# A scan solved by rounded and exact iterations: two rounded and one exact iteration per block in place of two and two, with another order inside a turn

## The reference

```python
def _mlp(params, h):
    W1, b1, W2, b2 = params
    return jax.nn.silu(h @ W1 + b1) @ W2 + b2
...
def step(params, kvt):
    k_t, v_t = kvt
    g = jax.grad(loss_fn)(params, k_t, v_t)
    new_params = tuple((p - LR * gp for p, gp in zip(params, g)))
    return (new_params, None)
params, _ = jax.lax.scan(step, (W1, b1, W2, b2), (k, v))
q = x @ W_Q
return _mlp(params, q)
```

## Time and profile before

| | |
|---|---|
| median of 3 runs | 483.13 us (482.81 to 485.1) |
| the profiled execution's own time | 484.08 us |
| its span, first to last instruction | 481.9 us |
| PE busy | 430.7 us, 89% of the span |
| DVE, ACT, POOL busy | 280.8, 245.1, 243.1 us |
| granted clock of PE, mean | 0.947 of full |
| turns of the scan | from 177.48 us (parameters of turn 0) to 327.6 us |

### The profile page before, as it was taken

The page is one execution under the profiler, slowest core; times in us unless marked ns, Lnnn a source line. Parts: engine busy times, 40 slices in busy tenths (PEclk is TensorE's granted clock), DMA queues, the critical chain, the costliest instruction groups (busy, mean ns, idle before and its releaser), DMA issues.

```text
span 481.9 us, 9866 instructions
## 1 busy us (share of the span) xinstructions
PE 430.7 (89%) x2875; PEld 356.0 (74%) x2875; DVE 280.8 (58%) x1031; ACT 245.1 (51%) x617; POOL 243.1 (50%) x369
## 2 busy tenths in 40 slices
PE   7899899999908989999999999999799799999940
PEld 5444699999903679899999989974644499999930
DVE  4945455555528646677777777754965245555514
ACT  3594355555410445556556565544696145555520
POOL 4367777545500344555555546552247777554530
PEclk9799999999957999999999999999989999999985
DMA  8981334100075200000000000000001417110028
GB/s 231 260 278 56 113 104 151 37 26 25 18 186 175 41 1 0 3 2 2 1 2 1 1 2 2 3 0 1 2 23 56 112 50 205 35 34 28 20 63 216
DMA packets 34513, 30.89 MB, mean 64 GB/s; under 512 B 3838, under 2 KB 30085, under 8 KB 34464
## 3 DMA queue, kind: packets, MB, share of 16 engines
q1 hardware_dynamic: 24608, 19.17, 14.7%
q0 software_dynamic: 4544, 8.47, 5.4%
q10 hardware_dynamic: 5312, 2.62, 2.1%
HBM read 15.55 MB, written 15.61 MB: 65 GB/s over the span
## 4 chain that ended last, share of the span: by engine, by line
PE 73%; DVE 8%; DMA 6%; POOL 4%; issue 4%; ACT 4%; ACTq 0%; SPq 0%; DVEq 0%; POOLq 0%
PE bank L1308 18%; PE bank L741 15%; PE bank L728 14%; POOL slots_dram L1435 3%; PE bank L599 3%; DMA stage<-y_dram 3%; PE bank L1101 2%; PE bank L689 2%; PE bank L716 2%; PE bank L1178 2%; DMA stage<-slots_dram 2%; PE bank L1139 1%; DVE stats L419 1%; PE bank L699 1%; PE bank L1162 1%
## 5 line engine op out<-in xcount | busy, mean ns | idle before, releaser
L1692 DVE TENSOR_TENSOR sq<-bank,relu 128x512 f32<-128x512 f32 x86 | 59.5, 692 | 84.2 <-ACT relu L839 84.0
L1440 POOL DMA_INDIRECT y_dram<-y_out,stage x78 | 76.9, 986 | 59.2 <-ACT y_out L865 52.6
L741 PE MATMUL bank<-proj_w,sq 128*128 x624 | 86.4, 281 | 2.8 <-DVE sq L1692 2.8
L728 PE MATMUL bank<-tileT,tile_w 128*128 128x128 f32 x624 | 83.2, 277 | 0.0
L1435 POOL DMA_INDIRECT slots_dram<-rows,slots x64 | 63.3, 990 | 35.0 <-DVE slots L535 15.2
L741 PEld LDWEIGHTS bank<-proj_w,sq 128*128 128x128 f32 x624 | 75.6, 191 | 6.5 <-issue 3.5
L839 ACT ACTIVATE relu<-bank 128x512 f32<-128x512 f32 x94 | 56.1, 596 | 45.4 <-PE bank L728 37.6
L728 PEld LDWEIGHTS bank<-tileT,tile_w 128*128 128x128 f32 x624 | 76.9, 195 | 0.0
L865 ACT ACTIVATE y_out<-bank,stage 128x128 f32<-128x128 f32 x78 | 28.7, 368 | 33.2 <-PE bank L741 33.2
L1303 POOL TENSOR_TENSOR sq<-sq,last_rows 128x128 f32<-128x128 f32 x32 | 14.7, 458 | 54.2 <-DVE sq L1279 54.2
L599 PE MATMUL bank<-ones 128*128 128x512 f32 x32 | 20.6, 790 | 15.4 <-DVE res L1743 12.6
(11 more groups left out here) (278 smaller groups left out, 1046.6 us busy)
## 6 DMA issues: line engine op xcount, KB each, us to landing
slots_dram<-pad SPq DMA_DIRECT2D x2, 2535.0 KB, 14.0
stage<-slots_dram SPq DMA_DIRECT2D x18, 260.0 KB, 4.4
fc_w<-experts SPq DMA_DIRECT2D x1, 2048.0 KB, 20.3
proj_w<-experts SPq DMA_DIRECT2D x1, 2048.0 KB, 24.0
stage<-y_dram SPq DMA_DIRECT2D x8, 256.0 KB, 5.5
stage<-y_dram ACTq DMA_DIRECT2D x8, 256.0 KB, 6.2
y_dram<-y_out,stage POOLq DMA_INDIRECT x78, 2.3
res<-x SPq DMA_DIRECT2D x4, 256.0 KB, 3.8
```

Source lines behind the costliest of these rows:

```text
L728: last = nc.tensor.matmul(bank[i % 2][:, f_cols], tile_w[:, i % 2, f_cols], tileT[:, (f * NQ + tile_q(i)) % 2, tile_cols(i)], start=True, ...
L741: last = nc.tensor.matmul(bank[4 + i % 2][:, 0:P], sq[:, i % 2, f_cols], proj_w[:, k, f_cols], start=j == 0, stop=j == FJ - 1)
L1440: nc.gpsimd.indirect_dma_start(y_dram.ap(), bass.IndirectOffsetOnAxis(tiles[:, t, P:P + 1].bitcast(U32), 0), y_out[:, t % YBUFS, :], None, ...
L1692: nc.vector.tensor_tensor(wide_of(i)[2], wide_of(i)[0][:], wide_of(i)[1], ALU.mult)\
```

## The change

The exact chain does one iteration per block. The rounded chain still does two in a turn, and the result of its second is the guess from which the exact one starts. The settling check changes with it: the gap is now that between the exact iteration and the last rounded one, a second gap, between the two rounded ones, is summed by three more operations on POOL per turn, and the flag asks whether the gap times the ratio of the two gaps is small enough. The first product of the exact iteration (`pe_again`) takes two passes in place of one. In each turn's order the rounded chain's calls now stand ahead of the exact chain's.

```diff
-TOL = 5e-5
+TOL = 1e-4
+GAP_LIMIT = 3e-3
...
-            late, early = [], []
-            for r in range(ROUNDS):
-                late.append(Step(final, ROUNDS * turn + r, turn + r, turn, r, late[-1] if r else earlier, r == 0))
+            late, early = Step(final, turn, turn, turn, turn % KEPT, earlier), []
+            for r in range(AHEAD):
                 early.append(Step(ahead, n + r, n + r, turn + 1, 1 + turn % 2 if r else 0, early[-1] if r else None))
...
-            mm(x.h_bank, old.chain.ed[:, old.to, 1, :], old.chain.kk[:, step.block, :], start=False)\
+            mm(x.h_bank, as_kind(step, old.chain.ed[:, old.to, 1, :]), x.kk[:, step.block, :], start=False)\
...
+            def gap_of_steps(turn):
+                old, new = (0 if turn else 1), 1 + (turn + 1) % 2
+                pool.wait_ge(ahead.d_done, FIRST_AHEAD + AHEAD * turn)
+                nc.gpsimd.tensor_tensor(step_gap, ahead_ed[:, new, 1, :].bitcast(F32), ahead_ed[:, old, 1, :].bitcast(F32),
+                                        ALU.subtract).then_inc(step_gap_made, 1)
...
+            def gap_of_last(turn):
+                pool.wait_ge(final.erows_done, turn + 1)
+                pool.wait_ge(final.d_done, turn + 1)
+                nc.gpsimd.tensor_tensor(gap, last_ed[:, turn % KEPT], ahead_ed[:, 1 + (turn + 1) % 2].bitcast(F32),
+                                        ALU.subtract).then_inc(gap_made, 1)
...
             for turn in range(NBLK):
                 late, early = turn_steps(turn)
+                gap_of_steps(turn)
                 if turn:
                     square_gap(turn)
+                if early:
+                    pool_slope(pool, early[0])
+                square_steps(turn)
+                pool_slope(pool, late)
+                if turn:
                     add_gap(turn)
-                pool_slope(pool, late[0])
-                if turn:
                     square_new(turn)
                 if early:
-                    pool_slope(pool, early[0])
+                    pool_slope(pool, early[1])
+                add_steps(turn)
                 if turn:
                     add_new(turn)
...
+                gap_of_last(turn)
...
+            dve_link(dve, nc.vector.tensor_scalar(left[:], nrm[:, 2:4], nrm[:, 3:4], None, ALU.mult), at)
+            dve_link(dve, nc.vector.tensor_tensor(good[:, 2:4], allowed[:], left[:], ALU.is_ge), at)
```

More of the change, by code:

```diff
@@ L1466, in square_new @@
             def square_new(turn):
+                new = last_ed[:, (turn - 1) % KEPT]
                 nc.gpsimd.tensor_tensor(new_sq, new, new, ALU.mult).then_inc(new_squared, 1)
@@ L1949, in _ @@
                 more = early and before
-                if before:
-                    pe_e_transposed(pe, before[1])
-                pe_first(pe, late[0], turn)
-                pe_again(pe, late[0])
+                if before and not early:
+                    pe.wait_ge(ahead.erows_done, before[1].n + 1)
+                pe_first(pe, late, turn)
                 if more:
                     pe_w1_sums(pe, before[1], ahead_upd1)
+                    pe_b1_sums(pe, before[1], ahead_upd1)
                     pe_w2_sums(pe, before[1])
-                pe_offset(pe, late[0], turn)
-                if more:
-                    pe_b1_sums(pe, before[1], ahead_upd1)
                     pe_w2t_sums(pe, before[1], ahead_upd2)
-                pe_old_guess(pe, late[0])
-                pe_aa(pe, late[0], turn)
-                pe_a_transposed(pe, late[0], turn)
-                pe_yrows(pe, late[0], turn)
                 if early:
@@ L1969, in _ @@
                     pe_first(pe, early[0], turn)
-                pe_y(pe, late[0], turn)
-                pe_th_transposed(pe, late[0])
-                pe_first(pe, late[1], turn)
+                pe_again(pe, late)
+                pe_offset(pe, late, turn)
+                pe_old_guess(pe, late)
                 if early:
+                    pe_aa(pe, early[0], turn)
+                    pe_y(pe, early[0], turn)
                     pe_offset(pe, early[0], turn)
-                    pe_aa(pe, early[0], turn)
@@ L1976, in _ @@
-                pe_inner(pe, late[0])
-                if early:
-                    pe_y(pe, early[0], turn)
                     pe_yrows(pe, early[0], turn)
-                pe_da_old(pe, late[0])
-                if early:
                     pe_th_transposed(pe, early[0])
-                pe_da(pe, late[0])
+                pe_aa(pe, late, turn)
+                pe_y(pe, late, turn)
+                pe_yrows(pe, late, turn)
                 if early:
                     pe_inner(pe, early[0])
-                pe_e_transposed(pe, late[0])
@@ L1987, in _ @@
-                pe_ee(pe, late[0])
-                pe_again(pe, late[1])
+                pe_a_transposed(pe, late, turn)
+                pe_th_transposed(pe, late)
                 if early:
+                    pe_first(pe, early[1], turn)
                     pe_da(pe, early[0])
-                    pe_first(pe, early[1], turn)
                     pe_e_transposed(pe, early[0])
-                pe_y_old(pe, late[1])
-                pe_a_transposed(pe, late[1], turn)
+                pe_inner(pe, late)
@@ L1995, in _ @@
+                pe_da_old(pe, late)
                 if early:
                     pe_again(pe, early[1])
[L1997 to L1998 removed]
+                pe_da(pe, late)
                 if early:
                     pe_offset(pe, early[1], turn)
+                    pe_old_guess(pe, early[1])
                     pe_aa(pe, early[1], turn)
[L2002 to L2006 removed]
@@ L2007, in _ @@
-                pe_da(pe, late[1])
-                if early:
-                    pe_th_transposed(pe, early[1])
-                pe_e_transposed(pe, late[1])
+                    pe_y(pe, early[1], turn)
+                    pe_yrows(pe, early[1], turn)
+                    pe_th_transposed(pe, early[1])
+                pe_e_transposed(pe, late)
+                pe_w1_sums(pe, late, upd1_done)
+                pe_b1_sums(pe, late, upd1_done)
+                if early:
+                    pe_inner(pe, early[1])
```

154 lines of the change are left out of this document (61 added, 93 removed).

## The result

The changed kernel takes **500.27 us** (median of 4 runs, 499.65 to 502.35) against 483.79 (4 runs) for the kernel before beside it: a ratio of 1.0348, 95% interval 1.0321 to 1.0375. It is slower: the profiled span grew by 16.9 us (481.9 to 498.8) where 8.2 was forecast.

What follows compares the result with a forecast made beforehand. PE's queue was taken to set the turn now, the rounded chain's loop after the change. Loop 4.9, turn 0 -1.0, last turn -1.7 and clock +6 sum to +8.2: median 491.3 us, range 475 to 500.

Steps and rivals of the forecast that it cites:

- the loop: Rounded chain, one weight update to the next: turn of 9.68 us, 0.38 longer than before; 13 turns cost +4.9 us.
- the clock: PE's granted clock falling in the thin stretch around the update: 6 of 13 turns, +6 us, between 0 and +13.
- the last turn with the check: Turn 15, exact chain only, once, up to the product of the norms: -1.7 us, with POOL's own queue late.
- `guess_rows` behind the copy: ACT, second silu to second `d`: `guess_rows` queued behind the copy to `last_ed`; 3.27 us against 3.14, 0.13 more.
- Step 2: First to second silu: targets behind tanh, exact passes ahead of `pe_inner`, exact `aa` ahead on DVE; 4.07 us against 3.83.
- step 4: Second `d` to the update: three exact parameters on DVE ahead of `ahead_ee`; 1.64 us against 1.38, 0.26 more.
- Turn 0: First turn, 11.71 us before with a clock fall: 10.7 with fewer passes, -1.0 us, between -2 and +0.4.
- B: Rival: the loop lengthens and the clock stays; 485.3 us, by itself 482 to 488, chance 0.20.
- C: Rival: the loop gets shorter as PE, with 56 passes, waits for the chain; turn 8.9, 474.4 us, chance 0.30.
- the prediction's reading: The skill's rule on PE idling briefly between matmul groups: each turn falls once, time 7 us above the sum.

Runs made afterwards that it cites:

- the run with three fillers: Changed kernel plus three products of ones (six passes, read by nothing) per turn on PE ahead of the rounded sums: 487.53 us, ratio 1.0072.
- both moves: Changed kernel with the masked product of the errors right behind the second `d` on DVE and `guess_rows` ahead of the `last_ed` copy on ACT: 472.57 us, ratio 0.9781.
- a third: On top of those two moves, the targets of the first rounded iteration on ACT ahead of its tanh: 470.09 us, ratio 0.9718.

## Why the prediction was off

It had the direction and the loop, and failed above all at one term, **the clock**: "Between no fall and one in each of 13 turns I take 6 of them". Ten of the 13 fell, one for twice as long, and they cost 11.6 us in place of 6. At 1.16 a falling turn the price of 1.0 was nearly right; the number of falls was not. Of the 8.7 us between the 8.2 forecast and the 16.9 measured, the clock in these turns is 5.6, what lies outside the scan 3.1, and the last turn with the check 1.4; the loop gives 1.4 back. The last turn of before, which I set against the falls, is a mean over 7.90 us, 6.48 of them busy; the stretch around the update has 2.37 of 3.40, and the row ahead of turn 0, 2.08 of 3.41 with a fall behind it, was the nearer one.

**The loop.** 9.58 against the 9.68 worked out. The four steps in the changed kernel's full-clock turn, mark at 316.79: to the first silu 0.78 (0.70 forecast), to the second 3.99 (4.07), to the second `d` 3.20 (3.27), to the update 1.62 (1.64). The names were right where they were tested alone: `ahead_ee` behind the exact parameters is worth 0.59 (so more than the 0.26 that the step had grown by), and `guess_rows` behind the copy 0.38. Step 2 came as worked out, with `pe_inner` 2.80 and the errors 3.24 behind the mark (319.59 and 320.03), for 2.83 and 3.24. But its names were not levers: the targets ahead of the tanh gave 0.09 a turn, and taking the six exact passes from ahead of `pe_inner` brought the errors forward by 0.20 and made the turn longer.

**What the two terms had in common.** I costed step 4's wait as 0.26 of the loop and the clock as a thing apart. The runs show the same 0.71 us of standing PE behind both: fill it and the falls end at an unchanged turn; remove it and the turn is shorter and all falls but one end.

**Turn 0**: -1.05 against -1.0, with one fall in it as taken. There is luck in that: in the run with six passes in the middle of the turn, whose program is the same up to the end of turn 0, this turn kept the clock and took 9.59 (178.25 to 187.84). **The last turn and the check**: -0.28 against -1.7. A fall between the last mark and the norms (clock 0.91 of that stretch) ate it; in the run with three fillers, without a fall there, the way is 18.68, 1.4 less than the 20.06 of before, and with both moves 18.31. PE waited 1.97 ahead of the product, as forecast over 1.5. **Outside the scan**: +3.1, where I had taken nothing. The programs are the same up to the first mark, and yet it lies anywhere from 177.27 to 179.90 in the kernels run here. From the norms to the end it is 149.9 to 153.7 us in them, and 151.59 before and 152.64 in the changed kernel lie within that. So both parts lie inside the spread of these kernels and needn't come from the change; what makes the spread no run here shows.

The rivals: B, the loop longer with the clock up, would be 485.3; the filler made that case, at 487.5. C, the loop shorter, failed for this kernel, but the orders on ACT and DVE named against it were what it needed, and without them it is 472.57, below its 474.4.

The Trainium skill's "TensorE: Matmul & The Clock Gate", section "A second HAM failure mode: psum-queue depth-cycling", describes a kernel whose PE idles briefly between groups of matmuls and whose clock swings between the two levels. The trace agrees, with 0.71 us of idling and ten of 13 turns with a fall. Read as one fall in each turn, which is the prediction's reading, it comes to 498.3, closer than my six; all 13 fell with `guess_rows` moved alone, but three of 13 kept the clock in the changed kernel.

## What to carry to other kernels

When work is taken off the engine that set the pace, look at what its queue had covered: a late operation on another engine that cost nothing behind a full PE becomes both a longer loop and a PE that stands still. Cost the clock at the thinnest stretch that the new order makes, and find that stretch before placing any filler; even so, in the order of before filler at the thinnest place that I had found did not end the falls. When an order is rewritten, put each engine's operation that the loop waits for ahead of those that nobody waits for; two single moves turned a change of +3.5% into one of -2.2%, and with a third it was -2.8%, with overlapping intervals. But look one step on for who waits for the operation that is put back: moving `pe_inner` ahead of the exact passes made the turn 0.36 longer (8.88 against 8.52).

## What the hardware showed that was not expected

Two passes a turn at the right place left seven of turns 1 to 13 with a fall, where there had been ten; six passes there left none, and six in the middle of the turn eight. Turns with the same work and the same 2.37 us busy of 3.40 around the update fell in some cases and not in others. In the order of before, one exact iteration less made a turn at full clock 0.3 us shorter and the kernel 14 us longer (498.43 against 484.29); the turns 1 to 13 of the profiled execution took 12.9 more, all by the clock.
